# Attention scores on tiles of 64 weight columns, and the next chunk's inputs turned one unit sooner

## The chip, the cores and the metric

The kernel runs on one core of a Trainium2 chip. The metric is the device time of one execution, in microseconds (us); lower is better. The core has TensorE for matmuls (PE in the profile, with its weight loads as PEld), VectorE (DVE), ScalarE (ACT), GpSimd (POOL) and SyncE (SP), which here only issues DMAs. Each engine runs its own stream of instructions in order; the streams meet at semaphores.

## The reference

The input is x, 8 batches of 1024 tokens of width 256, in fp32 (8192 rows). Six residual steps follow one another; each normalises its input first (layer norm without weights):

```python
x = x + 0.5 * L0_ffn(ln(x))     # fp4 block quantised gate/up/down, 704 hidden
x = x +       L0_attn(ln(x))    # linear attention, state decays by g per head
x = x + 0.5 * L0_ffn(ln(x))
x = x + 0.5 * L1_ffn(ln(x))     # ternary weights, 1024 hidden, exact gelu
x = x +       L1_attn(ln(x))    # linear attention with elu+1, plus four memories
x = x + 0.5 * L1_ffn(ln(x))
```

The first attention has 16 heads of width 16 and carries a 16x16 state per head over the tokens:

```python
state = gb * state + einsum('bhi,bhj->bhij', v_t, k_t)
y_t   = einsum('bhij,bhj->bhi', state, q_t)
```

The second computes `num = sq . cumsum(sk v)` and `den = sq . cumsum(sk)` in the same heads, divides, and mixes in what four fixed memories recall. The first feed-forward layer of the second kind is `gelu(x W1' + b1) W2' + b2` with W1, W2 rounded to -1, 0, 1 times a scale.

## The kernel before

x stays on the core as X, 64 tiles of 128 tokens by 256. Work goes through it in 16 chunks of four tiles (512 tokens), six stages one after the other, with the first steps of a stage laid over the end of the one before. Stage numbers S are 0 and 2 for the quantised feed-forward, 1 and 4 for the attentions, 3 and 5 for the ternary feed-forward. PE's arithmetic in fp32 is kept with high and low parts (XTH and XTL hold the turned input of a chunk, two buffers of 2 x 512 columns each); where both operands of a matmul are plain fp32, it is recorded as two pairs of weight load and multiply.

Both attentions work by blocks. A pass n handles one tile of 128 tokens, as two halves h of 64 tokens. Heads lie in two groups k of 128 rows, and each of these in four row groups q of 32 rows with two heads of 16 in each. KM (KM1 in the second) holds the keys masked by head: for each half h, 128 columns, the first 64 with the rows of the even heads and zeros elsewhere, the next 64 with those of the odd heads. So one score matmul takes 32 rows by 128 columns of KM as its weights and the 64 queries of QT (SQ in the second) as the moving side, and writes the scores of both heads, 128 partitions (head, key) by 64 queries. There are 2 x 2 x 4 = 16 such matmuls in a pass, order h, k, q, each q in a PSUM bank of its own.

In the first attention (`attn0_pe`) a pass on PE is: `attn0_front` (values and keys of tile n), `scores(n)` at L1096, `enter(m)` at L1114 for m = n-1 (the state from before the half, 32x32 tiles), `values(m)` at L1127 (masked scores times values, 128x32 tiles), `grow(n)` at L1145 (the new state, 64x32 tiles), the output projection of tile n-2 (L1169), and, in three passes of four, a part of the next chunk: its transposes (L264) and the projections of q, k (L46 to L48, `mm3`). DVE multiplies the scores by a table of decays (L1242), copies values and keys, and updates the state (L1253, L1260). Banks are handed out in a ring of six, in an order that a generator writes out (`slots0`); taking a bank waits for whoever reads its former content.

In the second (`attn1_pe`) it is: `values_keys(n)` (L46 to L48, transposes of the keys at L1704), `grow(m, 0)` (L1719), `values(m)` (L1733, L1739), `grow(m, 1)`, `scores(n)` (L1755), `enter(m)` (L1773, L1779), transposes of the results (L1818, L1824), `recall` of tile n-10 (L1790), parts of the next chunk and the output projection (L1837).

In the ternary feed-forward a chunk is eight units of 128 hidden columns each. `ffn1_unit` on PE: for unit m of the stage (f = m % 8) two weight loads, each with XTH and XTL (L1494, L1495) into one of two banks; then the down part of unit m-5 with the high and low half of the activation (L1511, L1513). ACT does gelu (L1528) and the high half (L1532), DVE the low half Hl (L1556). Inside unit f == 4 PE turns the inputs of the next chunk (`ffn1_turn`, eight transposes at L264 into banks 2 and 3), ACT copies them to XTH behind its own unit 4 (`turn_act`, L270), and DVE forms XTL behind its unit 6 (`low_dve`, L274). The next chunk's first unit waits for XTL (L1489). The normalised rows XN that are turned are written by ACT at units 5, 6, 7 and 0. At the start of the last stage, S == 5, unit m == 4 waits on PE for the end of the attention (`n_yte`, `s_xd`).

Of the kernel before, what the change touches and what calls it, by code (L numbers as in the profile page):

```python
# [25 lines left out]
def macaron(nc, x, wgu, wd, wqkv, bqkv, bv, wo0, bo0, gam, w1, b1, w2, b2, aw, awo, gate, mem, mnorm, cst, out):  # L26
    pwd = nc.dram_tensor("pw_scratch", [16, 256], F32, kind="Internal").ap()
    top = ExitStack()
    with top:
# [1046 lines left out]
        def attn0_pe(pe):  # L1076
# [9 lines left out]
            def scores(n):  # L1086
                w = (n // 4) % 2
                banks = [attn0_take(pe, "s", n, q) for q in range(4)]
                for h in range(2):
                    ts = slice(128 * (n % 4) + 64 * h, 128 * (n % 4) + 64 * h + 64)  # L1090
                    ks = slice(256 * (n % 4) + 128 * h, 256 * (n % 4) + 128 * h + 128)
                    for k in range(2):
                        for q in range(4):
                            gs = slice(32 * q, 32 * q + 32)
                            c = 128 * k + 64 * h
                            t = pe.matmul(banks[q][:, c:c + 64], KM[w][gs, k, ks], QT[w][gs, k, ts],  # L1096
                                          start=True, stop=True)
                            if h == 1 and k == 1:
                                t.then_inc(s_sc, 1)

            def enter(m):

# [373 lines left out]
        def ffn1_unit(pe, S, m):  # L1476
            tb = 64 * (S - 3)
            i, f = m // 8, m % 8
            if S == 5 and m == 0:
                for s, v in emptied1(*order1[(len(order1) - 1) // 3 * 3]):  # L1480
                    pe.wait_ge(s, v)
            if S == 5 and m == 4:
                pe.wait_ge(n_yte, NT)
                pe.wait_ge(s_xd, 64 * 5)
            if m < 8 * NS:
                F = 16 * S + i
                b = F % 2
                if f == 0:
                    pe.wait_ge(s_xl, 2 * F + 2)  # L1489
                if m > 1:  # L1490
                    pe.wait_ge(s_ge, tb + m - 1)
                fs = slice(128 * f, 128 * f + 128)
                for k in range(2):
                    pe.matmul(PS[m % 2][:, :], W1T[:, k, fs], XTH[b][:, k, :], start=(k == 0), stop=False)  # L1494
                    t = pe.matmul(PS[m % 2][:, :], W1T[:, k, fs], XTL[b][:, k, :], start=False, stop=(k == 1))  # L1495
                t.then_inc(s_u1, 1)
                if f == 4 and (i + 1 < NS or S == 3):
                    ffn1_turn(pe, S, i + 1)
            if m >= LAG:
                q = m - LAG  # L1500
                i, f = q // 8, q % 8
                v, w = i % 2, q % 8
                pe.wait_ge(s_hl, tb + q + 1)
                if S == 3 and q == 8:
                    pe.wait_ge(s_xd, 64 * 2 + NT)
                if f == 0 and i > 1:
                    pe.wait_ge(s_xd, 64 * S + 4 * (i - 2) + 4)
                for j in range(4):
                    o = PS[4 + 2 * v + j // 2][:, 256 * (j % 2):256 * (j % 2) + 256]
                    js = slice(128 * j, 128 * j + 128)  # L1510
                    pe.matmul(o, Hh[w][:, js], W2T[:, f, :], start=(f == 0 and j % 2 == 0), stop=False,  # L1511
                              skip_group_check=True)
                    t = pe.matmul(o, Hl[w][:, js], W2T[:, f, :], start=False, stop=(f == 7),  # L1513
                                  skip_group_check=True)
                t.then_inc(s_d1, 1)
# [5 lines left out]
        def ffn1_unit_act(act, S, m):  # L1521
# [10 lines left out]
            act.activation(Hh[w][:, :], Hf[u][:, :], ACT.Copy).then_inc(s_hh, 1)  # L1532
            if f == 0 and (0 < i < NS - 1 or i == NS - 1 and S == 3):
                norm(act, *chunk(16 * S + i + 1), (3,))
            if f == 4 and (i + 1 < NS or S == 3):
                if i > 0:
                    act.wait_ge(s_u1, tb + 8 * (i - 1) + 8)
                for k in range(2):
                    turn_act(act, 16 * S + i + 1, k, PS[2 + k])
# [11 lines left out]
        def ffn1_unit_dve(dve, S, m):  # L1551
            tb = 64 * (S - 3)
            i, f = m // 8, m % 8
            if m < 8 * NS:
# [3 lines left out]
                if f < 3 and (i + 2 < NS or i + 2 == NS and S == 3):  # L1558
                    for k in ((0, 1), (2, 3), (4, 5, 6, 7))[f]:
                        stats(dve, *chunk(16 * S + i + 2), k)  # L1560
                if f == 6 and (i + 1 < NS or S == 3):
                    if i > 0:
                        dve.wait_ge(s_u1, tb + 8 * (i - 1) + 8)
                    for k in range(2):
                        low_dve(dve, 16 * S + i + 1, k, PS[2 + k])
# [97 lines left out]
        def attn1_pe(pe):  # L1663
# [79 lines left out]
            def scores(n):  # L1743
# [3 lines left out]
                banks = [take("s", n, g) for g in range(2)]  # L1747
                for h in range(2):
                    ts = slice(128 * j + 64 * h, 128 * j + 64 * h + 64)
                    ks = slice(256 * j + 128 * h, 256 * j + 128 * h + 128)  # L1750
                    for k in range(2):
                        for q in range(4):
                            gs = slice(32 * q, 32 * q + 32)
                            c = 512 * (q % 2) + 128 * k + 64 * h
                            t = pe.matmul(banks[q // 2][:, c:c + 64], KM1[i % 2][gs, k, ks], SQ[i % 4][gs, k, ts],  # L1755
                                          start=True, stop=True)
                            if h == 1 and k == 1 and q % 2 == 1:
                                t.then_inc(n_sc, 1)

            def enter(m):  # L1760

# [426 lines left out]
```

## Time and profile before

| what | us |
|---|---|
| median of three runs | 2619.19 (2616.74 to 2619.5) |
| the profiled execution's own time | 2622.44 |
| its span, first to last instruction | 2620.5 |
| PE busy in the span | 2458.2 (94%) |
| DVE busy | 1867.1 (71%) |
| ACT busy | 1411.6 (54%) |
| POOL busy | 1271.0 (49%) |

Busy time of PE counts a matmul from its start to its modelled end; matmuls overlap in the pipe, so the distance between their starts says what one costs, and its duration says how long its result takes. A "slot" below is the time from the start of one block of matmuls to the start of the next.

### The profile page before, as it was taken

What the parts mean: (1) busy time and instruction counts of PE and PEld (TensorE: products, weight loads), DVE (VectorE), ACT (ScalarE), POOL (GpSimd) and SP (SyncE); (2) the same over time, 40 slices, a digit from 0 to 9 for tenths busy, and PEclk for the clock granted to TensorE, in tenths of its full rate; (3) what the DMA queues carried; (4) which work ended last, traced back from release to release, by engine and by line L of the source; (5) the groups of instructions that cost most, each with busy time, mean ns of one, the idle gap of its engine ahead of it and who ended that gap; (6) DMA issues with size and microseconds to landing.
All of it is one profiled execution on the core that took longest, in us unless ns stands there. A gap on an engine that the chain in (4) does not pass through costs nothing.

```text
span 2620.5 us, 77992 instructions
## 1 busy us (share of the span) xinstructions
PE 2458.2 (94%) x32232; PEld 2140.7 (82%) x32232; DVE 1867.1 (71%) x4326; ACT 1411.6 (54%) x2345; POOL 1271.0 (49%) x1382
## 2 busy tenths in 40 slices
PE   4999999999999989989998999989999999979999
PEld 3888888888888868878888888878888888858888
DVE  8999898567767789899985666545665556546664
ACT  4555555433343445545555888755444445428886
POOL 5878888612121158768886333113433444453221
PEclk9999999999999999999999999999999999979999
DMA  5000000000000010000000000000000000000001
GB/s 185 1 7 1 1 1 1 3 23 23 23 23 23 23 42 1 1 1 1 1 1 5 15 1 1 1 19 17 18 18 16 16 19 16 19 1 25 33 33 41
DMA packets 67566, 45.97 MB, mean 18 GB/s; under 512 B 13184, under 2 KB 66192, under 8 KB 67216
## 3 DMA queue, kind: packets, MB, share of 16 engines
q1 hardware_dynamic: 67216, 41.00, 5.6%
q8 instruction: 257, 4.21, 0.7%
q14 instruction: 93, 0.76, 0.1%
HBM read 15.78 MB, written 8.40 MB: 9 GB/s over the span
## 4 chain that ended last, share of the span: by engine, by line
PE 63%; issue 15%; POOL 11%; DVE 8%; ACT 3%; DMA 0%; POOLq 0%; DVEq 0%; ACTq 0%
PE ps L46 10%; PE ps L48 10%; PE ps L47 10%; PE ps L1494 4%; PE ps L1495 4%; PE ps L1513 4%; PE ps L1511 3%; PE ps L612 3%; PE ps L264 3%; PE ps L1169 3%; PE ps L1096 3%; DVE XTL L274 2%; POOL a1pry L2067 2%; POOL a1pry L2069 2%; POOL a1l L2055 2%
## 5 line engine op out<-in xcount | busy, mean ns | idle before, releaser
L1556 DVE TENSOR_TENSOR gHl<-gHf,gHh 128x512 fp32r<-128x512 f32 x256 | 191.3, 748 | 202.4 <-ACT gHh L1532 202.0
L231 POOL TENSOR_SCALAR ve<-mv 128x4 f32<-128x4 f32 x96 | 22.5, 234 | 613.2 <-DVE mv L221 609.0
L46 PE MATMUL ps<-WGH,XTH 128*128 128x512 f32 (+1 forms) x768 | 300.6, 391 | 12.1 <-DVE XTL L274 6.0
L48 PE MATMUL ps<-WGL,XTH 128*128 128x512 f32 (+1 forms) x768 | 290.7, 378 | 0.0
L47 PE MATMUL ps<-WGH,XTL 128*128 128x512 f32 (+1 forms) x768 | 290.1, 378 | 0.0
L826 POOL TENSOR_TENSOR fHTL<-fHTF,fHTH 128x768 fp32r<-128x768 f32 x128 | 236.8, 1850 | 83.1 <-ACT fHTF L691 83.1
L682 ACT ACTIVATE fSG<-ps 128x704 f32<-128x704 f32 x128 | 97.1, 759 | 331.3 <-PE ps L48 331.3
L1511 PE MATMUL ps<-W2T,gHh 128*128 128x256 f32 x1024 | 255.7, 283 | 0.0
L1513 PE MATMUL ps<-W2T,gHl 128*128 128x256 f32 x1024 | 253.0, 281 | 0.0
L46 PE MATMUL ps<-WDH,fHTH 128*128 128x256 f32 x768 | 224.6, 292 | 4.0 <-issue 4.0
L1528 ACT ACTIVATE gHf<-ps,B 128x512 f32<-128x512 f32 x256 | 176.1, 688 | 92.8 <-PE ps L1495 90.4
L1494 PE MATMUL ps<-XTH,W1T 128*128 128x512 f32 x512 | 206.1, 403 | 19.0 <-DVE XTL L274 18.0
L2055 POOL TENSOR_TENSOR a1l<-a1l,a1rc 128x128 f32<-128x128 f32 x128 | 49.7, 410 | 359.2 <-DVE a1rc L2022 359.2
L48 PE MATMUL ps<-WDL,fHTH 128*128 128x256 f32 x768 | 219.0, 285 | 0.0
L47 PE MATMUL ps<-WDH,fHTL 128*128 128x256 f32 x768 | 219.0, 285 | 0.0
L251 ACT ACTIVATE XN<-X,nb,rs 128x256 f32<-128x256 f32 x384 | 209.5, 590 | 9.8 <-POOL nb L237 9.8
L832 POOL TENSOR_TENSOR fV<-fH,frc 128x704 f32<-128x704 f32 x128 | 178.3, 1393 | 57.9 <-DVE frc L769 57.6
L1495 PE MATMUL ps<-XTL,W1T 128*128 128x512 f32 x512 | 203.0, 396 | 0.0
L1513 PEld LDWEIGHTS ps<-W2T,gHl 128*128 128x128 f32 x1024 | 192.7, 188 | 10.3
L1511 PEld LDWEIGHTS ps<-W2T,gHh 128*128 128x128 f32 x1024 | 192.1, 188 | 9.7
L838 POOL TENSOR_TENSOR fHX<-fV,fsc 128x704 f32<-128x704 f32 x128 | 178.0, 1390 | 28.0 <-DVE fV L306 28.0
L270 ACT ACTIVATE XTH<-ps 128x512 fp32r<-128x512 f32 x192 | 107.6, 593 | 120.2 <-PE ps L264 120.2
(239 smaller groups left out, 7104.0 us busy)
## 6 DMA issues: line engine op xcount, KB each, us to landing
X<-in_x SPq DMA_DIRECT2D x16, 512.0 KB, 8.8
a0vp<-a0vt SPq DMA_DIRECT2D x256, 32.0 KB, 2.2
a1vp<-a1vk SPq DMA_DIRECT2D x256, 32.0 KB, 2.2
out<-X SPq DMA_DIRECT2D x16, 512.0 KB, 2.9
tws<-in_w SPq DMA_DIRECT2D x2, 1024.0 KB, 7.6
WN<-in_wgu SPq DMA_DIRECT2D x3, 384.0 KB, 5.9
a0km<-in_wqkv SPq DMA_DIRECT2D x2, 384.0 KB, 3.2
a1pry<-in_aw SPq DMA_DIRECT2D x1, 768.0 KB, 4.5
```

Source lines behind the costliest of these rows:

```text
L46: e.matmul(o, hh, mh, start=first, stop=False)
L47: e.matmul(o, hl, mh, start=False, stop=False)
L48: return e.matmul(o, hh, ml, start=False, stop=last)
L251: t = act.activation(XN[:, j, :], X[:, 4 * i + j, :], ACT.Identity, scale=rs[b][:, j:j + 1], bias=nb[b][:, j:j + 1])
L826: pool.tensor_tensor(HTL[(n - 3) % 2][:, :, :], HTF[:, :, :], HTH[(n - 3) % 2][:, :, :].bitcast(F32), ALU.subtract).then_inc(s_hlo, 1)
L832: pool.tensor_tensor(s3(V[n % 2][:, :]), s3(H[n % 2][:, :]), cast16(rc[n % 2][:, :], 44), ALU.mult).then_inc(s_hv, 1)
L838: pool.tensor_tensor(s3(HX[(n - 1) % 2][:, :]), s3(V[(n - 1) % 2][:, :]), cast16(sc[(n - 1) % 3][:, :], 44), ALU.mult).then_inc(s_hx, 1)
L1494: pe.matmul(PS[m % 2][:, :], W1T[:, k, fs], XTH[b][:, k, :], start=(k == 0), stop=False)
L1495: t = pe.matmul(PS[m % 2][:, :], W1T[:, k, fs], XTL[b][:, k, :], start=False, stop=(k == 1))
L1511: pe.matmul(o, Hh[w][:, js], W2T[:, f, :], start=(f == 0 and j % 2 == 0), stop=False, skip_group_check=True)
L1513: t = pe.matmul(o, Hl[w][:, js], W2T[:, f, :], start=False, stop=(f == 7), skip_group_check=True)
L1556: dve.tensor_tensor(Hl[m % 8][:, :], Hf[m % 4][:, :], Hh[m % 8][:, :].bitcast(F32), ALU.subtract).then_inc(s_hl, 1)
```

## The change

In both `scores` each matmul is split in two: b = 0 takes the 64 columns of KM of the even heads and writes partitions 0 to 63, b = 1 the 64 columns of the odd heads and writes partitions 64 to 127. The order is h, k, b, q. There are 32 matmuls in a pass, on tiles of 32 rows by 64 columns, with the same 64 moving columns. Semaphores rise at the last matmul of each bank, as before.

In the ternary feed-forward `ffn1_turn` moves from unit f == 4 to f == 3 on PE, ACT's two copies from its unit 4 to its unit 3, and DVE's two subtractions from its unit 6 to its unit 5. The wait at the start of the last stage moves from ahead of unit 4 to within unit 3, between its up part and the transposes.

```diff
--- before.py
+++ after.py
@@ -1088,15 +1088,16 @@
                 banks = [attn0_take(pe, "s", n, q) for q in range(4)]
                 for h in range(2):
                     ts = slice(128 * (n % 4) + 64 * h, 128 * (n % 4) + 64 * h + 64)
-                    ks = slice(256 * (n % 4) + 128 * h, 256 * (n % 4) + 128 * h + 128)
                     for k in range(2):
-                        for q in range(4):
-                            gs = slice(32 * q, 32 * q + 32)
-                            c = 128 * k + 64 * h
-                            t = pe.matmul(banks[q][:, c:c + 64], KM[w][gs, k, ks], QT[w][gs, k, ts],
-                                          start=True, stop=True)
-                            if h == 1 and k == 1:
-                                t.then_inc(s_sc, 1)
+                        for b in range(2):
+                            for q in range(4):
+                                gs, rows = slice(32 * q, 32 * q + 32), slice(64 * b, 64 * b + 64)
+                                ks = 256 * (n % 4) + 128 * h + 64 * b
+                                c = 128 * k + 64 * h
+                                t = pe.matmul(banks[q][rows, c:c + 64], KM[w][gs, k, ks:ks + 64], QT[w][gs, k, ts],
+                                              start=True, stop=True)
+                                if h == 1 and k == 1 and b == 1:
+                                    t.then_inc(s_sc, 1)
 
             def enter(m):
 
@@ -1479,9 +1480,6 @@
             if S == 5 and m == 0:
                 for s, v in emptied1(*order1[(len(order1) - 1) // 3 * 3]):
                     pe.wait_ge(s, v)
-            if S == 5 and m == 4:
-                pe.wait_ge(n_yte, NT)
-                pe.wait_ge(s_xd, 64 * 5)
             if m < 8 * NS:
                 F = 16 * S + i
                 b = F % 2
@@ -1494,7 +1492,10 @@
                     pe.matmul(PS[m % 2][:, :], W1T[:, k, fs], XTH[b][:, k, :], start=(k == 0), stop=False)
                     t = pe.matmul(PS[m % 2][:, :], W1T[:, k, fs], XTL[b][:, k, :], start=False, stop=(k == 1))
                 t.then_inc(s_u1, 1)
-                if f == 4 and (i + 1 < NS or S == 3):
+                if S == 5 and m == 3:
+                    pe.wait_ge(n_yte, NT)
+                    pe.wait_ge(s_xd, 64 * 5)
+                if f == 3 and (i + 1 < NS or S == 3):
                     ffn1_turn(pe, S, i + 1)
             if m >= LAG:
                 q = m - LAG
@@ -1532,7 +1533,7 @@
             act.activation(Hh[w][:, :], Hf[u][:, :], ACT.Copy).then_inc(s_hh, 1)
             if f == 0 and (0 < i < NS - 1 or i == NS - 1 and S == 3):
                 norm(act, *chunk(16 * S + i + 1), (3,))
-            if f == 4 and (i + 1 < NS or S == 3):
+            if f == 3 and (i + 1 < NS or S == 3):
                 if i > 0:
                     act.wait_ge(s_u1, tb + 8 * (i - 1) + 8)
                 for k in range(2):
@@ -1558,7 +1559,7 @@
                 if f < 3 and (i + 2 < NS or i + 2 == NS and S == 3):
                     for k in ((0, 1), (2, 3), (4, 5, 6, 7))[f]:
                         stats(dve, *chunk(16 * S + i + 2), k)
-                if f == 6 and (i + 1 < NS or S == 3):
+                if f == 5 and (i + 1 < NS or S == 3):
                     if i > 0:
                         dve.wait_ge(s_u1, tb + 8 * (i - 1) + 8)
                     for k in range(2):
@@ -1747,15 +1748,16 @@
                 banks = [take("s", n, g) for g in range(2)]
                 for h in range(2):
                     ts = slice(128 * j + 64 * h, 128 * j + 64 * h + 64)
-                    ks = slice(256 * j + 128 * h, 256 * j + 128 * h + 128)
                     for k in range(2):
-                        for q in range(4):
-                            gs = slice(32 * q, 32 * q + 32)
-                            c = 512 * (q % 2) + 128 * k + 64 * h
-                            t = pe.matmul(banks[q // 2][:, c:c + 64], KM1[i % 2][gs, k, ks], SQ[i % 4][gs, k, ts],
-                                          start=True, stop=True)
-                            if h == 1 and k == 1 and q % 2 == 1:
-                                t.then_inc(n_sc, 1)
+                        for b in range(2):
+                            for q in range(4):
+                                gs, rows = slice(32 * q, 32 * q + 32), slice(64 * b, 64 * b + 64)
+                                ks = 256 * j + 128 * h + 64 * b
+                                c = 512 * (q % 2) + 128 * k + 64 * h
+                                t = pe.matmul(banks[q // 2][rows, c:c + 64], KM1[i % 2][gs, k, ks:ks + 64],
+                                              SQ[i % 4][gs, k, ts], start=True, stop=True)
+                                if h == 1 and k == 1 and b == 1 and q % 2 == 1:
+                                    t.then_inc(n_sc, 1)
 
             def enter(m):
```

## Rows read from the trace of the kernel before

**Rows 1.** The page: busy us (share) xinstructions; the instruction queue of PE.

```profile
PE 2458.2 (94%) x32232; PEld 2140.7 (82%) x32232; DVE 1867.1 (71%) x4326; ACT 1411.6 (54%) x2345; POOL 1271.0 (49%) x1382
...
q8 instruction: 257, 4.21, 0.7%
```

**Rows 2.** Stages: us, busy us (xinstructions) of PE, PEld, DVE, ACT, POOL; clock, DMA, GB/s.

```profile
520.00:935.00 415.00, 398.17 (x9044) 340.00 (x9043) 298.41 (x982) 153.10 (x279) 71.15 (x122) 0.99 0.10 23
...
1706.00:2300.00 594.00, 571.44 (x13760) 488.63 (x13759) 345.21 (x853) 286.55 (x528) 221.99 (x352) 0.99 0.07 17
2345.00:2620.00 275.00, 260.42 (x1660) 232.09 (x1658) 157.68 (x335) 211.76 (x343) 73.83 (x117) 0.99 0.10 32
```

**Rows 3.** PE in order of time, a pass of the first attention: start, us, what.

```profile
702.13 1.12 PE L1096 MATMUL ps<-a0qt,a0km 32*128 32x64 f32 x32
703.18 0.65 PE L1114 MATMUL ps<-a0qp,a0S 32*32 32x64 f32 x32
703.76 0.76 PE L1127 MATMUL ps<-a0A,a0vp 128*32 128x64 f32 x32
704.45 0.45 PE L1145 MATMUL ps<-a0vt,a0kp 64*32 64x32 f32 x32
704.83 1.13 PE L1169 MATMUL ps<-a0wo,a0YT 128*128 128x256 f32 x4
```

**Rows 4.** The chain that ended last, around 645: start, us, what.

```profile
644.89 0.35 PE ps L1145 x23
645.24 1.13 issue
```

**Rows 5.** Busy time between the ends of three stalls, columns as in rows 2.

```profile
646.36:690.73 44.37, 43.06 (x995) 37.09 (x995) 32.46 (x102) 14.47 (x27) 7.30 (x12) 1.00 0.10 23
690.73:699.42 8.69, 7.27 (x125) 6.10 (x126) 5.38 (x21) 3.94 (x6) 1.71 (x4) 1.00 0.07 17
```

**Rows 6.** DMA queues in the stretch 643.75 to 643.80.

```profile
q8 instruction: 1, 0.02, 158.4%
```

**Rows 7.** Busy time over 224 instructions before two edges, columns as in rows 2.

```profile
642.73:644.99 2.26, 2.26 (x117) 2.03 (x115) 1.99 (x6) 1.53 (x4) 0.44 (x2) 1.00 0.13 31
...
2119.32:2121.92 2.60, 2.60 (x126) 2.42 (x119) 0.89 (x4) 0.52 (x1) 2.45 (x4) 1.00 0.10 25
```

**Rows 8.** Groups by line, first attention: busy us, mean ns, idle before.

```profile
L1145 PE MATMUL ps<-a0vt,a0kp 64*32 64x32 f32 x1888 | 31.1, 232 | 9.9 <-issue 8.0 <-DVE a0kp L1229 1.7
```

**Rows 9.** PE in order of time, a pass of the second attention.

```profile
2015.77 0.46 PE L1719 MATMUL ps<-a1vp,a1vk 128*32 128x36 f32 x16
...
2019.63 0.25 PE L1773 MATMUL ps<-a1sq,a1S 32*32 32x64 f32 x3 [0.35 <-issue]
...
2020.09 0.55 PE L1818 MATMUL ps<-ident,a1nu 128*128 128x128 f32 x3
```

**Rows 10.** Waits in the two attentions: engine line, who, us, times, longest.

```profile
PEld ps L1145 <- issue: 9.8, 11, 1.5
...
PEld ps L1127 <- issue: 3.0, 2, 1.6
...
PEld ps L1779 <- issue: 3.4, 9, 0.7
PEld ps L1773 <- issue: 3.3, 7, 0.7
```

**Rows 11.** Busy time after a stall; the last but two is the granted clock.

```profile
737.61:741.02 3.41, 3.41 (x26) 2.79 (x27) 1.61 (x7) 0.00 (x0) 0.00 (x0) 0.50 0.11 24
```

**Rows 12.** All engines in order of time, an edge of chunks in the last feed-forward.

```profile
2427.32 1.28 DVE L274 TENSOR_TENSOR XTL<-ps,XTH 128x512 fp32r<-128x512 f32 x2
...
2427.83 0.28 PE L1513 MATMUL ps<-W2T,gHl 128*128 128x256 f32 x1
...
2428.66 0.50 PE L1494 MATMUL ps<-XTH,W1T 128*128 128x512 f32 x1 [0.55 <-DVE XTL L274]
```

**Rows 13.** The page, groups by line: the first matmul of a unit.

```profile
L1494 PE MATMUL ps<-XTH,W1T 128*128 128x512 f32 x512 | 206.1, 403 | 19.0 <-DVE XTL L274 18.0
```

## The prediction

> **What bounds the kernel now.** I read first the page's busy shares and its table of DMA queues [rows 1]: TensorE (PE) is busy 94% of the span. Then busy time by stage [rows 2]: in the first attention (520 to 935 us) PE works 398 of 415 us and VectorE (DVE) 298; in the second (1706 to 2300) PE 571 of 594 and DVE 345; in the last feed-forward PE 260 of 275. So a microsecond taken from PE's own stream is worth nearly a microsecond, as long as nothing takes its place. Third, the order of PE's work in one pass of the first attention [rows 3]: block after block starts where the last one drains, and nobody waits for data. Last the stretches where PE stands and the profile names no releaser ("issue"), for the change adds instructions exactly there.
>
> **Where the instructions come from.** An fp32 matmul is two load-and-multiply pairs, four instructions: the 16 score matmuls of a pass show as x32 pairs [rows 3]. The page's instruction queue made 257 transfers, 4.21 MB, so 16 KB each, for PE's 2 x 32,232 recorded instructions: 251 per transfer [rows 1]; with waits, which aren't counted as work, about 256. Now the stalls. In [rows 4] PE stops inside a block: 23 of 32 pairs of L1145, 1.13 us of "issue", then the rest. From the end of this stall (646.36) to the end of one at 690.73, [rows 5] count 995+995 instructions, and to the next (699.42) 125+126: 8 and 1 times 250. The stalls lie whole transfers apart: PE has run out of instructions at a transfer's edge. The transfer for the edge of [rows 4] starts after 643.75 [rows 6], and PE goes on at 646.36, 2.6 us later. When it is asked for can't be seen; I put it some 224 instructions ahead of the edge. Those 117+115 took 2.26 us, from 642.73 on [rows 7], so it went on 3.6 us after that point; at another edge 126+119 instructions took 2.60 us and PE had no stop [rows 7], so there it had 2.6 us or less. I take 3.0 us between these ends, nearer to the lower, which more of the edges show (an estimate from these rows). Hence the rule that I use: **an edge costs 3.0 us less the time in which PE ran the 224 instructions before it**.
>
> The Trainium skill (Runtime: NRT & Kernel Launch, Instruction fetch mechanics) describes refills in blocks of 16 KiB but calls the cost of crossing a boundary mostly hidden. The block size agrees with the page's row; the hiding doesn't, by the 1.13 us of [rows 4]. By that sentence the second step below would be nothing, which is rival 1.
>
> **Step 1, scores shorter.** Now 32 pairs take a slot (start to next block's start) of 703.18-702.13 = 1.05 us, while the 32 pairs of L1114, 32 columns of weights and the same 64 moving, take 0.58 [rows 3]: the wide weight load is the difference. After: 64 pairs on 32x64 tiles, eight tiles side by side. The nearest row with eight tiles at once is L1145 (64x32): 32 pairs busy 0.45 us, of which the last matmul is 0.23, so 0.22/31 = 7 ns from pair to pair [rows 3, 8]. Then 63x7 ns = 0.44 us, and some 0.19 us until the next block starts: 0.63 us. Bounds: 0.55 us, if the drain is that of L1145; 1.05 to 1.2 us, if the two column halves of a row group take turns. I take 0.63, since L1127 too runs four column tiles in parallel (32 pairs in 0.69 us [rows 3]). Gain 0.42 us x 64 passes x 2 attentions = **-54 us** (-64 to +10). Number of blocks that drain is the same as before. Eight semaphore increments of scores stay on the last multiply of each group; DVE's reads come as before. DVE needs 298/64 = 4.7 us of a pass of 6.5, so it doesn't become the bound.
>
> **Step 2, 64 more instructions in each pass.** The first attention has 9044+9043 instructions in 64 passes, the second 13760+13759 [rows 2]: with waits about 290 and 435 per pass, afterwards 354 and 499; edges: 73 and 109 before, 89 and 125 after.
> First attention: L1096, L1114, L1127, L1145 are 256 instructions in 2.70 us; the other 34 take the remaining 3.8 us. Only when an edge falls near the end of that run are there 224 instructions in under 3.0 us: some 44 places of 290, by the rule up to 0.9 us each; what is lost there now is 9.8+3.0 = 12.8 us [rows 10]. After, the run is 320 instructions in 2.28 us. An edge at its end has 224 instructions in 1.75 us behind it, one after 224 has 1.4; so 96 places, and about 20 more in which the loss fades: 116 of 354. 89 x 0.33 x 1.3 us = 38 us; +25.
> Second attention: from the first L1719 to the end of L1779 there are 352 instructions in 2020.09-2015.77 = 4.32 us, less a stall of about 0.6: 3.7 us [rows 9]. 224 of them take 2.4 to 2.6 us: just about the pace of supply, and what is lost is 3.4+3.3 = 6.7 us [rows 10]. After: 416 in 3.3 us; 224 that include the scores take 1.5 to 1.9 us. About 210 places of 499: 125 x 0.42 x 1.25 us = 66 us; +59.
> Together **+84 us**, between +55 (data there after 2.6 us) and +110 (after 3.4 us). The change thus packs more instructions into a stretch that is already at the edge of supply, and gets back less than nothing from the shorter slots: -54+84 = +30.
>
> **Step 3, clock.** A stall in the first attention ended at 737.61 with TensorE at 0.50 of its clock, that is 1.2 GHz, for 3.4 us [rows 11], in which 1.7 us are lost. The stall of [rows 4] brought no drop. With some 50 more stalls of about 1.3 us I add three drops: **+5 us** (0 to +20).
>
> **Step 4, inputs turned a unit sooner.** Once in each chunk PE waits at the first matmul of the next chunk for the low half XTL: last L1513 at 2427.83, next due 0.12 later, started 2428.66: 0.71 us [rows 12]. It happens 15 times in each of the two feed-forwards; the page has 18.0 us of idle time for it [rows 13], which counts from the modelled end of the last matmul, 0.16 us after the point where the next could have started: 18.0+30x0.16 = 22.8 us. XTL is done at 2428.60, since DVE starts it at 2427.32, after the difference Hl of unit 6 [rows 12]. Moved to unit 5 it comes one unit of PE's work (4 x 0.23 + 8 x 0.12 = 1.9 us) sooner, near 2426.7, 1.2 us before it is due: the wait goes entirely. What is moved: eight transposes on PE (same count, another place), two copies on ScalarE (ACT), two subtractions, 1.28 us, on DVE [rows 12]; nothing on SP or POOL. ACT has 212 of 275 us of work [rows 2], so the gelu behind the copies is late in one unit as now, one unit sooner; PE takes gelu's banks alternately and unit 5 instead of unit 6 needs it. Hl of unit 6 then follows the subtractions within 0.1 us. What is late next is ACT, with (275-212)/16 = 3.9 us a chunk in hand. At the start of the last feed-forward the wait for the end of the attention moves from unit 4 to unit 3, but behind unit 3's own matmuls, so it is held up only if the last residual add is over 3 us late: nothing. **-22 us** (-23 to -10).
>
> **Sum.** The profiled run has its own time of 2622.4 us (span 2620.5). 2622.4-54+84+5-22 = 2635.4. The median of the runs is 3.2 us below the profiled one, so **2632 us**.
>
> **Rivals.**
> 1. The supply keeps up, so the change is faster. It decides by when the next 256 instructions are there: at 1.4 us after the asking no edge in the longer runs costs anything, at 3.0 each costs what step 2 says. Fully hidden, only -54-22 = -76 would be left: 2543. Against it stand [rows 4, 10]. Chance 0.10. A milder form: they are asked for earlier while PE's queue is full, and an edge in a run costs 0.7 us less, (29+53) x 0.7 = 57 less: 2575 to 2600 with the bounds of step 1. For it: in the second attention 9+7 gaps [rows 10] stand for some 30 edges that fall in the last third of the run. Chance 0.22.
> 2. The column halves take turns (slot 1.05 to 1.1 us). Step 1 is worth 0; the instructions are more but come slower, so edges cost +45 rather than +84: 2619+45-22+5 = 2647. Against it L1127 and L1145. This is also the case in which the change doesn't do what it says. Chance 0.12.
> 3. Clock. Every third long stall drops the clock, with 1.7 us each: +25 on top of the forecast, 2657. Chance 0.08. It decides by the length of the stalls: from a length a little over the 1.13 us of [rows 4], which brought none.
> The forecast, slower because of supply, has 0.45, over 2612 to 2655; 0.03 is for others.
>
> **Chances and range.** A measurement can tell about 0.2% (5 us). Faster: 0.10+0.22 and the low end of the forecast, 0.04: 0.36. Same: 0.10 of the forecast and 0.03 of the rest: 0.13. Slower: 0.31+0.12+0.08 = 0.51. The range 2580 to 2660 leaves out rival 1's pure form and the end of rival 3. The forecast's own range is 2612 to 2655.
>
> **What would show it.** Step 1: slot of L1096's and L1755's successors (64 pairs) at 0.63 us where no "issue" falls in it. Step 2: the instruction queue has 273 transfers; "issue" inside L1114, L1127, L1145, L1773, L1779, L1790 sums to about 100 us instead of 20, at counts that are multiples of 250. Step 4: no wait of L1494 for XTL. Wrong it would be if "issue" stays under 40 us, or if the slot stays at 1.05.

## The result

The changed kernel takes 2653.6 us (median; 2641.5 to 2658.9) against 2619.4 us (2616.7 to 2621.1) of the kernel before: a ratio of 1.0125, 95% interval 1.0087 to 1.0163. It is slower beyond the noise, by 34 us (1.3%) where 13 were forecast; the time lies inside the range of 2580 to 2660. The profiled executions are 2650.0 us (after) and 2622.4 us (before), so what the two traces can explain is 27.6 us.

The page of the changed kernel: busy us (share) xinstructions, PE's instruction queue, and the group that was [rows 13], one line number lower now.

```profile
PE 2447.2 (92%) x36328; PEld 2125.7 (80%) x36328; DVE 1861.3 (70%) x4326; ACT 1412.5 (53%) x2345; POOL 1271.4 (48%) x1382
...
q8 instruction: 289, 4.73, 0.8%
...
L1492 PE MATMUL ps<-XTH,W1T 128*128 128x512 f32 x512 | 202.6, 396 | 1.9 <-ACT gHf L1529 1.2
```

PE has 4096 more pairs and 32 more transfers of 16 KB than in [rows 1], is busy 11 us less, and yet ends later. The wait for XTL of [rows 13], 18.0 us, is gone.

Where the time went shows when each stage is cut out by itself. Below, the first and the second attention, then the last feed-forward (S = 5) and the one of S = 3 (us, PE busy us (xinstructions), granted clock, DMA share, GB/s); the edges are each kernel's own: first score matmul to last output projection, and first to last matmul with W1. First the kernel before.

```profile
518.10:940.20 422.10, 405.10 (x9185) 0.98 0.10 23
...
1706.00:2345.70 639.70, 603.36 (x13983) 0.97 0.07 16
2345.70:2609.60 263.90, 253.66 (x1610) 0.99 0.09 30
1414.30:1689.30 275.00, 262.84 (x1702) 1.00 0.02 5
```

The changed kernel:

```profile
520.00:971.40 451.40, 403.49 (x11233) 0.97 0.09 22
...
1724.80:2386.60 661.80, 599.68 (x16031) 0.97 0.07 16
2386.60:2637.20 250.60, 249.14 (x1610) 1.00 0.10 32
1444.90:1707.70 262.80, 259.36 (x1703) 1.00 0.02 5
```

The attentions are 29.3 and 22.1 us longer, the last feed-forward is 13.3 us shorter, and that of S = 3 is 12.2 us shorter. In the first attention PE's idle time goes from 17.0 to 47.9 us (length less busy), 30.9 more: all of the stage's loss. Who is named for it (the list of waits, 500 to 975 us; engine line, who, us, times, longest):

```profile
PE ps L1128 <- issue: 21.1, 16, 2.0
...
PE ps L1146 <- issue: 15.3, 14, 1.6
...
PE ps L1115 <- issue: 4.4, 3, 2.2
```

and in the second attention (1690 to 2376 us):

```profile
PE ps L1781 <- issue: 15.7, 12, 1.9
...
PE ps L1775 <- issue: 6.1, 5, 1.9
```

One of these stalls in order of time (start, us, what):

```profile
712.70 0.91 PE L1097 MATMUL ps<-a0qt,a0km 32*64 32x64 f32 x64
713.54 0.65 PE L1115 MATMUL ps<-a0qp,a0S 32*32 32x64 f32 x32
714.12 0.61 PE L1128 MATMUL ps<-a0A,a0vp 128*32 128x64 f32 x22
716.31 0.40 PE L1128 MATMUL ps<-a0A,a0vp 128*32 128x64 f32 x10 [1.58 <-issue]
```

PE stops after 22 of the 32 pairs of one block, waiting for no engine and no data. From the end of this stall to the end of the next one, at 728.85, and from there to the end of one at 750.46 (busy time, columns as in [rows 2]):

```profile
716.31:728.85 12.54, 10.86 (x377) 9.22 (x376) 8.50 (x28) 4.20 (x9) 2.80 (x4) 1.00 0.11 25
728.85:750.46 21.61, 20.63 (x501) 17.11 (x500) 13.72 (x46) 8.05 (x14) 4.50 (x8) 0.92 0.09 22
```

753 and 1001 instructions: 3 and 4 times 250, as in [rows 5]. With what the view doesn't count as busy work (every record of PE in the trace), the step is 256. I went through all stalls over 0.3 us inside the short-matmul blocks of both kernels: 25 before (19.1 us), 61 after (79.9 us), and each of the 86 stands at a record number 256m + 449, with m a whole number. Counted stage by stage they are 13.6 us before and 48.0 after in the first attention, 6.2 and 33.5 in the second; counted a little differently, these add up to 0.7 and 1.6 us more than the totals.

The transfer for the edge at 716.31 starts here (queue, transfers, MB, share, in 713.75 to 713.80):

```profile
q8 instruction: 1, 0.02, 162.6%
```

PE goes on 2.5 us later. Over all stalls of the first attention this distance is 2.2 to 2.95 us, median 2.5; the transfer itself has ended 1.2 to 1.6 us before PE goes on. So how long PE has to wait once the transfer has started is known; what varies is how late the transfer starts: with 196 of the 256 instructions still to run at one edge and with 26 at another.

The Trainium skill (Runtime: NRT & Kernel Launch, Instruction fetch mechanics) calls the crossing of such a boundary mostly hidden, because instructions are issued more slowly than the buffer fills. It gives a block 256 instructions, and with that this trace agrees to the instruction. The hiding holds in the ternary feed-forwards, where PE is held up over 0.3 us at no edge of either trace, and not in the blocks of short matmuls, with 80 us of stalls at the boundaries.

### The profile page after: what moved, and what is told of

The parts are those of the page before. It is cut to its first block, busy times and chain, and to the rows that moved or that the text cites. A ratio compares the mean times of both kernels' runs of the same rounds, so it can differ in the third digit from the quotient of the medians.

```text
span 2648.0 us, 86184 instructions
## 1 busy us (share of the span) xinstructions
PE 2447.2 (92%) x36328; PEld 2125.7 (80%) x36328; DVE 1861.3 (70%) x4326; ACT 1412.5 (53%) x2345; POOL 1271.4 (48%) x1382
## 4 chain that ended last, share of the span: by engine, by line
PE 65%; issue 16%; POOL 11%; DVE 6%; ACT 2%; DMA 0%; SPq 0%; POOLq 0%; DVEq 0%; ACTq 0%
PE ps L46 10%; PE ps L48 10%; PE ps L47 10%; PE ps L1514 5%; PE ps L1512 4%; PE ps L1493 4%; PE ps L1492 4%; PE ps L612 3%; PE ps L1170 3%; PE ps L264 3%; PE ps L1097 2%; PE ps L1128 2%; POOL a1pry L2069 2%; POOL a1pry L2071 2%; POOL a1l L2057 2%
## 5 line engine op out<-in xcount | busy, mean ns | idle before, releaser
L231 POOL TENSOR_SCALAR ve<-mv 128x4 f32<-128x4 f32 x96 | 22.1, 231 | 613.6 <-DVE mv L221 609.5
```

## Experiments

"Wide" scores are the 16 matmuls of a pass with 128 weight columns, recorded as 32 pairs; "narrow" ones are those of the change, 64 pairs with 64 columns. An "edge" is the place, once in 256 instructions, where a new transfer's instructions begin. A "cover" is work of PE behind which a wait for another engine doesn't show.

### ffn_only: the feed-forward part alone

```diff
-            if S == 5 and m == 4:
-                pe.wait_ge(n_yte, NT)
-                pe.wait_ge(s_xd, 64 * 5)
...
+                if S == 5 and m == 3:
+                    pe.wait_ge(n_yte, NT)
+                    pe.wait_ge(s_xd, 64 * 5)
-                if f == 4 and (i + 1 < NS or S == 3):
+                if f == 3 and (i + 1 < NS or S == 3):
                     ffn1_turn(pe, S, i + 1)
```

with the same step on ScalarE (4 to 3) and VectorE (6 to 5).

> The kernel before with the feed-forward part of the change alone: the next chunk's inputs are turned after unit 4's matmuls instead of unit 5's, scores stay wide. Theory (the wait for XTL goes in both sizes of the last feed-forward and nothing takes its place, the rest of the change is untouched by it): about 25 us less than the kernel before, 2594 us, and inside the two feed-forwards the same 12 to 13 us each as in the changed kernel. Rival (part of what the stages show in the changed kernel comes from where the instruction edges happen to lie there): 15 us or less, with one of the two feed-forwards short of 10 us. The attentions should show their 13.6 and 6.2 us of stalls as before.

2587.8 us against 2618.5, ratio 0.9886 (0.9870 to 0.9902): 31 us faster. The two feed-forwards are 12.2 and 13.2 us shorter, as in the changed kernel, so this part isn't touched by the other. The remaining 5 us of the 31 aren't explained by this part. Its profile has 7 us less in the first attention, at a mean clock of 1.00 where the kernel before had 0.98: one stretch at half clock there, 3.4 us long, where the kernel before has three of together 13.7 us, and 2 us less of stalls. Whether its other executions had that too isn't known.

```profile
518.80:933.80 415.00, 400.84 (x9184) 1.00 0.10 24
```

### scores_only: both score parts, without the feed-forward part

The diff is that of the change, without its feed-forward lines.

> The kernel before with both score parts of the change and without the feed-forward part. Theory (instruction supply: 256 instructions per transfer, stalls at their edges): about 51 us over the kernel before, 2670 us; score slot 0.84 us instead of 1.05, stalls inside the dense runs about 80 us instead of 19, every one at a count of 256m+449 recorded instructions of PE. Rival 1 (the loss of the changed kernel comes from PE's clock alone, and the stalls are its effect): stalls would lie anywhere in the count, and the loss would go with the half-clock stretches. Rival 2 (the two parts disturb each other): the time would be under 2650 or over 2690 us.

2672.4 us, ratio 1.0210 (1.0188 to 1.0232): 54 us slower, with 51 expected. Score slot 0.843 us in both attentions, 60 stalls of together 73.8 us, all at records 256m + 449. The two parts add up to +54 - 31 = +23; the change measured +34, with +23 to +43 as its interval, so a remainder of some 10 us is neither shown nor excluded. Rival 1 (clock first) falls with the places of the stalls; rival 2 falls with the time.

### spread_wide: wide scores, another order in the first attention

```diff
                     scores(n)
                 if n == 0:
                     pe.wait_ge(s_xd, NT)
+                if n >= 2:
+                    bank = attn0_take(pe, "o", n - 2)
...
                 if 0 <= m < NT:
                     enter(m)
                     values(m)
                 if n < NT:
                     grow(n)
-                if n >= 2:
-                    bank = attn0_take(pe, "o", n - 2)
...
```

The whole block of the projection moves, four long matmuls with a slot of 0.78 us in the kernel before; the order of banks and VectorE's residual add move with it. The query projections, which the expectation names beside it, stay where they were in this edit.

> The kernel before, scores wide as there, with one change of order in the first attention: the output projection of tile n-2, and the query projections with it, are done between the scores and the transposes and state matmuls instead of after them, so that the long run of short matmuls (256 instructions in 2.7 us) is cut in two by work of some 2 us with few instructions. Theory (a stall comes where the 224 or so instructions ahead of an edge ran in less than the transfer takes): the 13.6 us of stalls of the first attention fall to under 5, and 10 to 15 us are gained: 2605 us, with two half-clock stretches fewer. Rival (the stalls come from the number of instructions or from their kind, not from how densely they follow): the stalls stay at 10 to 16 us and the time at 2619, or it is slower by new waits of PE for banks that VectorE and ScalarE free later.

2628.7 us, ratio 1.0040 (1.0025 to 1.0055): slower by 10, not faster by 13. The stage and its waits:

```profile
520.20:948.20 428.00, 410.52 (x9185) 1.00 0.10 23
```

```profile
PEld ps L1114 <- issue: 21.2, 63, 0.7
PEld ps L1096 <- issue: 14.2, 63, 0.5
PEld ps L1164 <- ACT a0km L1060: 11.9, 15, 0.8
```

The cause is confirmed, the gain is not. Stalls at edges fall from 13.6 to 0.6 us with the very same instructions (x9185 in both) and the clock goes from 0.98 to 1.00: the order of the instructions makes the stalls, not their number or kind. That they follow too densely ahead of an edge fits; it isn't the whole of it, as step 2 of the account below shows. Two covers are gone. L1114, whose weight load used to run on behind the scores, starts afresh behind a long matmul (63 times, 0.3 us each). And once in a chunk the projection waits for its bank (15 times, 11.9 us): in the ring of six it takes the one of the last key projection, and ScalarE is still copying the masked keys of the next chunk out of it. In order of time, one of these waits:

```profile
565.42 1.46 ACT L1060 ACTIVATE a0km<-ps,a0bm,a0par 128x512 f32<-128x512 f32 x2
...
566.93 1.13 PE L1164 MATMUL ps<-a0wo,a0YT 128*128 128x256 f32 x4 [0.66 <-ACT a0km L1060]
```

The row of L1096 is no loss of this kernel; the one before has it too. The restart I had at nothing; waits for banks stood in the rival, without a price.

### spread_narrow: the same order, with narrow scores in the first attention

> The same order of the first attention, with the score part of the change in the first attention alone (64 pairs on 32x64 tiles); the second attention and the feed-forward are as in the kernel before. The number of instructions is that of the changed kernel in this stage. Theory (density ahead of an edge): stalls of the first attention under 15 us instead of the 48 of the changed kernel, score slot 0.84 or less instead of 1.05, so 64 x 0.2 = 13 us less than the run above: 2592 to 2605 us. Rival (64 more instructions in each pass have a price of their own wherever they stand, some 0.5 us a pass): stalls near 48 us again and the time at 2640 or more.

2634.4 us, ratio 1.0055 (1.0038 to 1.0071).

```profile
518.60:953.50 434.90, 403.48 (x11232) 1.00 0.10 23
```

The stage has the changed kernel's 11232 pairs and is 16.5 us shorter; its stalls are 16.1 us in place of 48.0. The rival (64 instructions cost the same wherever they stand) is refuted. The time is 29 us over the top of its range; 24 of them are what the run above had missed already. Against the kernel above, slots give back 13 us and stalls take 15.5, and the stage is 6.9 us longer: even with the run cut, narrow scores gain nothing in this order.

### split: the scores in two halves, with the output projection between

```diff
-                    scores(n)
+                    banks = scores(n, 0, None)
                 if n >= 2:
                     bank = attn0_take(pe, "o", n - 2)
...
+                if n < NT:
+                    scores(n, 1, banks)
```

> The kernel spread_narrow with its scores of the first attention cut in two: 32 pairs of head half 0, then the output projection of tile n-2 (four long matmuls), then 32 pairs of half 1, directly ahead of the state and value matmuls. Same instructions, same count, another place. Theory on the slot (PE takes the first 40 or so pairs from a queue that was filled while long matmuls ran, at 7 ns a pair, and then goes at the pace at which instructions come, 16.6 ns a pair): each half starts behind long matmuls, runs at 7 ns, and takes 0.35 to 0.45 us, 0.75 to 0.85 us for both. Rival (16.6 ns comes from the tiles or banks of the second half of the pairs): the second half takes 0.6 us, the first 0.25 to 0.35. Theory on the stalls (density ahead of an edge): the run that isn't interrupted grows from 96 to 128 pairs, so the stalls rise from 16 us to some 25, below the 48 of the changed kernel; time 2635 to 2645. Rival (count alone): 16 us as in spread_narrow.

2640.5 us, ratio 1.0087 (1.0066 to 1.0107), from two executions. This one is about the slot. In order of time:

```profile
711.14 0.49 PE L1097 MATMUL ps<-a0qt,a0km 32*64 32x64 f32 x32
711.56 1.13 PE L1164 MATMUL ps<-a0wo,a0YT 128*128 128x256 f32 x4
712.62 0.49 PE L1097 MATMUL ps<-a0qt,a0km 32*64 32x64 f32 x32
713.04 0.65 PE L1116 MATMUL ps<-a0qp,a0S 32*32 32x64 f32 x32
```

Both halves have a slot of 0.42 us (711.56 - 711.14; 713.04 - 712.62), 0.27 from first to last pair. In one piece of 64 pairs the last pair starts at 0.696 us: 0.27 for the first 32, 0.43 for the second 32, where single pairs follow at 8.5 and 17 ns instead of 7. (The expectation put the change at pair 40 or so; it comes at the 33rd.) The second half is as quick as the first as soon as long matmuls stand ahead of it, so its tiles and banks are not what slows it; its place behind 32 other pairs is. That PE works off a queue which was filled during the long matmuls, and then runs at the pace at which instructions reach it, fits, but no row shows that queue, so this reason is argued and not shown.

On the stalls neither theory held: they fell from 16.1 to 9.7 us, with the run grown from 96 to 128 pairs, where mine had 25 and the rival 16. So the length of the run alone doesn't set them; that 64 score pairs in one piece do harm of their own fits, and wasn't tried by itself. The time is in the forecast range, but not for the forecast reason: the stage is 5.7 us longer than in spread_narrow (440.6) although stalls fell by 6.4, and the projection's wait for its bank grew by 6.1 (21.1 us after 15.0).

### front_w: values and keys projected behind the scores

```diff
                 if n < NT:
-                    if n:
-                        attn0_front(pe, n)
                     scores(n)
+                    if n:
+                        attn0_front(pe, n)
```

with its two waits for the chunk's projections left ahead of the scores, and its bank behind theirs.

> The kernel before with one other change of order in the first attention: the projection of V and the two transposes of K of tile n are done behind the scores of tile n instead of ahead of them, so that work of 1.1 us with few instructions cuts the run of 256 instructions after the first 64; wide scores. Theory (density): stalls of the first attention from 13.6 to under 4 us, as in spread_wide, without the waits for ScalarE's copy that cost that kernel its gain; a restart of some 0.3 us in at most one pass of two (10 us at the most, 5 more likely); 2605 to 2615. Rival (cover gone): the product with VectorE's decayed keys now comes 1.3 us behind the transposes instead of 2.3 and waits for VectorE in most passes, 0.3 us or more each: 2625 or more, though the stalls are gone.

2614.5 us, ratio 0.9988 (0.9978 to 0.9997): 4 us faster, in the forecast range. No stall at an edge is left in the stage.

```profile
518.70:935.40 416.70, 409.72 (x9185) 1.00 0.10 23
```

```profile
PEld ps L1097 <- issue: 19.7, 60, 0.4
PEld ps L1115 <- issue: 10.9, 64, 0.3
PEld ps L1128 <- DMA a0vp<-a0vt: 4.6, 7, 0.9
```

Restarts (the first line is 5 us more than in the kernel before, the second is new, in every pass) and the values' DMA, asked for 1 us later, eat most of the 13.6 us: the stage is 5.4 us shorter. The rival (waits for VectorE's decayed keys) is not there: 1.2 us.

### best_w1 and best_n1: state matmuls of the second attention moved back

```diff
-                if 0 <= m < NT:
+                if n >= NT and 0 <= m < NT:
                     enter(m)
...
                 if n < NT and r >= 0:
                     recall(r)
+                if 0 <= m and n < NT:
+                    enter(m)
```

> The kernel with the feed-forward part alone, and in the second attention the state matmuls of tile n-1 (128 instructions) moved behind the recall, the transposes and the turns of inputs, ScalarE's copy of the numerators moved accordingly; scores wide. Theory (density): the 4.5 us of stalls in the second attention shrink to 1 or 2, nothing else changes: 2582 to 2588. Rival (cover gone): the numerators reach ScalarE 2 us later and the transposes of the next tile wait for them: 2595 or more.

> The same with the score part of the change in the second attention alone. Theory (density): the slot gives 64 x 0.2 = 13 us, stalls of the second attention are under 15 us instead of the 28 to 33 of the kernels with narrow scores in the old order: 2578 to 2592. Rival (64 more instructions in a pass cost what they cost wherever they stand): stalls near 30 us, 2603 or more.

Both contain the feed-forward part, and both lose it: 2644.3 us (ratio 1.0103, 1.0086 to 1.0120) and 2646.0 us (1.0107, 1.0088 to 1.0126). Stalls at edges in the second attention are 0.3 us with wide scores and 13.6 with narrow ones, as expected; the stage grew all the same by 52 and 58 us over the 637.3 of ffn_only. The waits of best_w1 in the stage (the same three take 0.2, 14.0 and 7.1 us in ffn_only):

```profile
PEld ps L1790 <- DVE a1A L1965: 38.0, 41, 1.0
...
PEld ps L1704 <- ACT a1km L1880: 24.0, 15, 2.4
...
PE ps L1824 <- POOL a1pry L2077: 20.2, 20, 2.3
```

The recall (L1790) needs the bank of scores that VectorE is just masking; the 1.0 us of state matmuls between them had been its cover. The time is the rival's (2595 or more), but the rival looked for it in the numerators' way to ScalarE, and the largest new wait is this one.

### best_fw, best_fn, best_ln: what can be combined

best_fw is ffn_only with the order of front_w; best_fn adds narrow scores in the first attention; best_ln has wide scores there, narrow ones in the second, and the three transposes of the numerators between scores and state matmuls.

> The feed-forward part and the order of front_w (V's projection and K's transposes of the first attention behind the scores), scores wide in both attentions. Theory (the two act in different stages and add): 2587.8 - 4 = 2584 us, between 2580 and 2587; stalls of the first attention under 1 us. Rival (the 7 us by which the first attention was shorter in the profile of the feed-forward part alone than in the kernel before belong to that part): they would be lost or doubled, under 2578 or over 2590.

> The same with the score part of the change in the first attention alone. Uninterrupted runs are then 64 and 96 pairs in a pass, as in spread_narrow. Theory (density): slot 0.84 instead of 1.05 gives 13 us, stalls of the first attention 10 to 16 us as in spread_narrow, 2580 to 2590, so no better than the kernel above; a gain only if the stalls stay under 8. Rival (supply no matter once the order is broken): 2571.

> best_fw with the score part of the change in the second attention, and there the three transposes of the numerators of tile n-2 between scores and state matmuls (0.4 us of work with 6 or so instructions) instead of behind them. Theory (density): 13 us from the slots, but 0.4 us break the run too little: stalls in the second attention of 18 to 28 us against the 28 to 33 of the kernels with narrow scores and 4.5 with wide ones; 2585 to 2597. Rival (any cut of the run ends the stalls): under 8 us of them and 2575.

2587.9 us (0.9887, 0.9871 to 0.9904), 2584.5 us (0.9878, 0.9863 to 0.9893) and 2621.8 us (1.0021, 1.0011 to 1.0032). best_fw is 1 us over its range of 2580 to 2587: on top of the feed-forward part the order of front_w gained nothing. Its first attention takes 416.3 us without a stall, and that of ffn_only took 415.0 with some 12 us of them. best_fn has the lowest time of all; its interval overlaps those of ffn_only and best_fw, and these can't be told apart. The first attention of best_fn, against the 416.7 us of front_w:

```profile
518.50:930.50 412.00, 399.82 (x11232) 1.00 0.10 24
```

It is 4.7 us shorter, with stalls of 6.8 us, under the 8 that the expectation had set for a gain. Up to 1.7 us of it are a stretch at half clock that only front_w has there. So by the profiles narrow scores gain some 3 us once work with few instructions follows them at once; the times don't show it clear of the noise. In best_ln the stalls of the second attention were 24.7 us, inside the 18 to 28 expected, but the time was 25 us over the top of my range. The stage is 675.0 us long, 36 more than in best_fw, of which stalls less slots explain 7. The state matmuls now start afresh behind the transposes (L1778), and PE waits in three places for the bank of the transposes, which ScalarE empties (a1l) only behind its copy of the next numerators (waits, 1690 to 2330 us):

```profile
PEld ps L1778 <- issue: 17.4, 69, 1.5
...
PEld ps L46 <- ACT a1l L1918: 6.4, 15, 0.5
...
PEld ps L1850 <- ACT a1l L1918: 4.8, 10, 0.5
PEld ps L264 <- ACT a1l L1918: 4.0, 9, 0.5
```

The density theory gave the stalls right here and the time wrong, by lost covers as in spread_wide and best_w1. It had the stalls too high in split (25 us against 9.7) and in best_fn (10 to 16 against 6.8).

## Why the prediction was right, and where it wasn't

**What bounds the kernel.** Held: 30.9 us more idle time of PE inside the first attention made it 29.3 us longer.

**Where instructions come from.** Held, more exactly than I had it: the edges of all 86 stalls lie whole multiples of 256 records apart. In the last part I named 273 transfers as the sign; that was a slip of division. 2 x 4096 instructions are 32 transfers, 289, as found.

**Step 1, slot.** The mechanism held (eight tiles side by side, 7 ns a pair), the size didn't: 0.843 us instead of 0.63, so 128 x 0.207 = 26.5 us instead of 54. The term of the sum that failed is "63 x 7 ns": L1145, from which I took it, has 32 pairs only, and the 7 ns end after 32: the first 32 pairs take 0.27 us, the others 0.43. The rows of before showed no run of 64 such pairs, and my bounds (0.55 to 1.2) did hold it. Rival 2's time (2647) came near, but its cause isn't there: the slot isn't 1.05, and in split 32 pairs of both column halves start within 0.27 us, so the halves don't take turns.

**Step 2, supply.** +84 us forecast, +61 measured (79.9 - 19.1). By stage it was +25 against 34.4, and +59 against 27.3 (by the stage counts): the total was as near as it was because two errors partly cancelled. That is luck, not the rule. The rule "3.0 us less the time of the 224 instructions before" is not how it works. Worked out over the edges that really came, it gives 29 us in the first attention of the changed kernel where 48 were lost, and 50 in the second where 37 (with the stalls between blocks) were; in split and spread_narrow it gives 12 and 5 where 10 and 16 were lost. Seven stalls of the first attention, together 10.8 us, follow 224 instructions that took more than 3 us; four of them (8.3 us, one of 2.3 that ended at 628.79) stand in L1115 or L1128 soon behind the 64 score pairs, with transfers that started when fewer than 50 instructions were left. What holds is the second part of it: PE goes on 2.2 to 2.95 us after the transfer starts. What decides when it starts is open; no view shows the request.

**Step 3, clock.** The sign held. TensorE runs at half clock (1.2 GHz) for 86 us of the kernel before and 111 us of the changed one, most of it in stretches of 3.4 us; at most half of the 25 us is lost, 12.6, where I took 5 (0 to 20). Seven such stretches are in the first attention of the changed kernel, where the one before had three and the orders with few stalls (spread_wide, spread_narrow, front_w, best_fn) have one or none; ffn_only, with 12 us of stalls, has one as well. The row after a stall that ended at 784.18:

```profile
784.30:787.70 3.40, 3.40 (x57) 2.70 (x58) 1.50 (x7) 0.38 (x1) 0.00 (x0) 0.52 0.10 24
```

**Step 4, inputs.** Held: XTL is done 0.80 us before it is due (1.2 in the forecast), and a chunk takes 15.86 us instead of 16.70. In order of time, around the chunk's edge at 2433.03:

```profile
2430.36 0.68 DVE L1557 TENSOR_TENSOR gHl<-gHf,gHh 128x512 fp32r<-128x512 f32 x1
2430.95 1.28 DVE L274 TENSOR_TENSOR XTL<-ps,XTH 128x512 fp32r<-128x512 f32 x2
...
2433.03 0.39 PE L1492 MATMUL ps<-XTH,W1T 128*128 128x512 f32 x1
2433.49 0.39 PE L1492 MATMUL ps<-XTH,W1T 128*128 128x512 f32 x1
```

Each edge of chunks gave 0.84 us instead of 0.76, and the two stages together 25.5 in place of 22.8: I had priced only the wait for XTL (18.0) of the 19.0 us of idle time in [rows 13]; for the other 1.7 us I have no row.

**Sum.** By the sizes that were measured: -26.5 + 60.8 - 25.5 + (0 to 12.6) = +9 to +21, plus 2 to 3 us of slots that grew beside (the recall's from 0.753 to 0.778 us). The traces differ by 27.6, so 4 to 16 us are not assigned. The forecast was +13 with -54 + 84 + 5 - 22. Slower is right for the reason given. That the size lies in its range is partly luck: a gain that was 27 us smaller and a loss that was 23 us smaller cancel.

**Rivals.** The milder form of supply keeping up (0.22) described the second attention alone: 27 us there, where the forecast had 59. The pure form fell to 80 us of stalls. The clock rival was too dear: 25 us on top of the 5 in the forecast, where at most 12.6 were lost in all, and in the first attention seven of some 35 stalls over 0.3 us, not every third, brought the clock down. That its total of 2657 lies nearest to the measured 2654 is luck.

## What to carry to other kernels

Count instructions as well as time. Where PE runs 200 or more short instructions in a stretch of 2 us, as it does here, further ones were not free even though each matmul was shorter. A look at whether the stalls called "issue" stand a fixed number of instructions apart tells it before anything is built. Cutting such a run with work of few instructions removed the stalls or most of them, but what was moved had covered something: price the restart of every block behind a long matmul (0.2 us in front_w, 0.3 in spread_wide) and find who is late for the moved one, or the gain is gone. And a change of several parts should be measured in parts: here the one that gained 31 us was hidden under one that lost 54.

## What the runs showed of the hardware

- Pairs of 32-row, 64-column tiles start every 7 ns within groups of eight, with one pause of 60 ns and then pauses of 12 ns between the groups, for 32 pairs (0.27 us); the next 32, behind a pause of 58 ns, follow at 8.5 to 17 ns (0.43 us). Behind long matmuls the count starts anew (0.27 us for each 32 in split).
- From the start of an instruction transfer that PE waits for until PE goes on it takes 2.2 to 2.95 us. It started with anything from 26 to 196 instructions left. In both traces, over all edges, none started more than 300 instructions ahead of its edge, so never much more than one block ahead.
- In the first attention of the changed kernel the clock fell to half right behind seven stalls of 1.6 to 2.2 us, and not behind others as long (1.8 us, ended at 716.31; 2.0 us, at 542.61; 2.3 us, at 628.79); in spread_wide, without them, 420 us ran at full clock.
- The times of the two kernels with the most such stalls spread most: 17 us over four executions of the changed kernel and 14 over four of scores_only, against 4 to 10 us over four executions of the others.
